# A routed two-layer network inside an attention kernel: expert units of 256 rows instead of 512, four to a chunk

## What is computed

```python
h = tokens(x)                                    # (32, 1024, 64)
h = layernorm(h + attention(h))                  # one head, softmax over 1024 keys
logits = h @ gate_w + gate_b                     # 8 experts
e = argmax(softmax(logits)); prb = softmax(logits)[e]
pos = running count of rows of expert e          # over all 32768 rows in order
kept = pos < C                                   # C = 1.25 * 32768 / 8
y = relu(h @ w1[e] + b1[e]) @ w2[e] + b2[e]      # 64 -> 256 -> 64
out = layernorm(h + nan_to_num(y * prb * kept))
```

## Time and profile before

| | us |
|---|---|
| median of 3 runs | 1235.28 (1235.03 to 1239.02) |
| the profiled execution, device time | 1234.83 |
| its span, first to last instruction | 1233.0 |
| TensorE busy | 1041.4 (84%), 5036 instructions |
| VectorE busy | 919.1 (75%) |
| ScalarE busy | 650.8 (53%) |
| POOL busy | 718.3 (58%) |
| mean granted TensorE clock | 0.938 |

### The profile page before, as it was taken

The page is one execution under the profiler, slowest core; times in us unless marked ns, Lnnn a source line. Parts: engine busy times, 40 slices in busy tenths (PEclk is TensorE's granted clock), DMA queues, the critical chain, the costliest instruction groups (busy, mean ns, idle before and its releaser), DMA issues.

```text
span 1233.0 us, 17442 instructions
## 1 busy us (share of the span) xinstructions
PE 1041.4 (84%) x5036; PEld 534.8 (43%) x5036; DVE 919.1 (75%) x1927; ACT 650.8 (53%) x880; POOL 718.3 (58%) x712
## 2 busy tenths in 40 slices
PE   3899999999999999999999999999989873345530
PEld 2455555555455555555554555554544431111210
DVE  4667778778989898988888988888888664535541
ACT  2355554555666666666666666666656541223320
POOL 0014555444676767666766676767675776536655
PEclk9999999999999999999999999999999976677775
DMA  5334433444444444444444443434351202222300
GB/s 122 88 77 124 105 91 76 111 112 100 106 109 107 106 102 107 105 106 104 105 106 109 99 117 94 123 93 124 76 126 35 70 16 75 74 61 72 89 12 2
DMA packets 102661, 112.02 MB, mean 91 GB/s; under 512 B 54350, under 2 KB 78919, under 8 KB 102566
## 3 DMA queue, kind: packets, MB, share of 16 engines
q1 hardware_dynamic: 85158, 93.78, 31.5%
q0 software_dynamic: 17408, 17.12, 4.6%
HBM read 42.20 MB, written 19.30 MB: 50 GB/s over the span
## 4 chain that ended last, share of the span: by engine, by line
PE 55%; DVE 25%; issue 9%; another core or an unknown queue 5%; ACT 2%; DMA 1%; POOL 1%; SPq 1%; POOLq 0%; DVEq 0%; ACTq 0%
PE p_u L562 15%; PE p_st L546 8%; DVE mx L929 8%; PE p_st L549 7%; PE p_sm L532 5%; PE p_misc L518 4%; PE p_misc L497 4%; PE p_misc L577 3%; PE p_misc L623 3%; PE p_misc L638 2%; DVE ld L980 1%; DVE b_o L1135 1%; DVE b_p L1084 1%; DVE b_n L1100 1%
## 5 line engine op out<-in xcount | busy, mean ns | idle before, releaser
L1263 POOL DMA_INDIRECT slots<-rows,idx x256 | 265.0, 1035 | 236.1 <-issue 147.2
L1275 POOL DMA_INDIRECT out<-b_o,b_ix x288 | 304.3, 1056 | 138.7 <-issue 77.6
L929 DVE TENSOR_REDUCE mx<-p_sm 128x1 f32<-128x1024 f32 x252 | 307.3, 1219 | 89.8 <-PE p_sm L532 82.5
L751 ACT ACTIVATE pT<-p_st 128x1024 f32<-128x1024 f32 x256 | 262.1, 1024 | 186.7 <-PE p_st L549 98.9
L562 PE MATMUL p_u<-pT,vv 128*64 128x512 f32 x1024 | 263.5, 614 | 0.0
L546 PE MATMUL p_st<-mQ,sK 128*128 128x512 f32 x512 | 183.6, 440 | 5.3 <-ACT pT L751 3.4
L549 PE MATMUL p_st<-mR,sR 72*128 72x512 f32 x512 | 161.1, 395 | 0.0
L532 PE MATMUL p_sm<-sK,mQ 64*128 64x512 f32 x252 | 139.9, 555 | 12.8 <-DVE mx L929 8.2
L532 PE MATMUL p_sm<-hi,mQ 64*128 64x512 f32 x252 | 139.8, 555 | 0.0
L546 PEld LDWEIGHTS p_st<-mQ,sK 128*128 128x128 f32 x512 | 79.4, 189 | 104.2 <-issue 79.4
L623 PE MATMUL p_misc<-b_xT,b_w 64*128 64x512 f32 x244 | 79.3, 730 | 34.1 <-issue 19.2
(11 more groups left out here) (181 smaller groups left out, 1492.8 us busy)
## 6 DMA issues: line engine op xcount, KB each, us to landing
mQ<-hi SPq DMA_DIRECT2D x64, 256.0 KB
b_in<-slots SPq DMA_DIRECT2D x72, 132.0 KB
b_x<-slots SPq DMA_DIRECT2D x72, 128.0 KB
sK<-hi SPq DMA_DIRECT2D x32, 256.0 KB
sK<-lo SPq DMA_DIRECT2D x32, 256.0 KB
mR<-lo SPq DMA_DIRECT2D x32, 256.0 KB
sR<-hi SPq DMA_DIRECT2D x32, 256.0 KB
xt<-in_x SPq DMA_DIRECT2D x32, 196.0 KB
```

Source lines behind the costliest of these rows:

```text
L751: act.activation(pT[k % 4][:, :], flat(p_st), ACT.Exp).then_inc(exp_done, 1)
L929: dve.tensor_reduce(mx[:, p, j:j + 1], flat(max_place(n, j)), AX.X, ALU.max).then_inc(max_done, 1)
L1263: pool.indirect_dma_start(slots, bass.IndirectOffsetOnAxis(ap=idx[:, p, j:j + 1], axis=0), rows[:, p, j, :], None, bounds_check=SLOTS - 1, ...
L1275: pool.indirect_dma_start(out_rows, bass.IndirectOffsetOnAxis(ap=b_ix[:, o, j:j + 1], axis=0), b_o[:, o, j, :], None, bounds_check=T - 1, ...
```

## The change

UNIT becomes 256 and a chunk holds four units (two pairs, v = 0 and 1), so a chunk still has 1024 rows. The last units of the experts are filled better, and NC = (128 + 8) / 4 = 34. HOST begins at step 6: 27 chunks inside steps 6 to 32, 7 after the attention (27 and 28 from the table of image 30, then 29 to 33). The first chunk takes its units from image 2's table, written in step 4. Each chunk now reads four table entries and issues 16 DMAs; `up` and `down` run twice as many matmuls of 256 columns; `rectify` does eight activations of 256 columns instead of four of 512 and waits for both pairs before the first; `sums_copy` does two instead of one. The tiles b_w1 and b_w2 get room for two pairs. Transposes, VectorE's work on a chunk and the scatters of a chunk keep their count and size. The diff, cut to its core:

```diff
-UNIT = 512
+UNIT = 256
+PAIRS = 2
+CT = PAIRS * UT
-NC = (NB * S // UNIT + E) // 2
-HOST = [*range(8, NB + 1)]
+NC = (NB * S // UNIT + E) // 4
+HOST = [*range(6, NB + 1)]
@@ image_of
     for n in (NB - 4, NB - 2):
-        if c < n - 3:
+        if c < n - 1:
             return n
-TAKEN = [2 * IMAGE.count(n) for n in TABLES]
+TAKEN = [4 * IMAGE.count(n) for n in TABLES]
@@ load_chunk
-                for u in range(2):
-                    named = sp.value_load(tab[0:1, 2 * c + u:2 * c + u + 1], min_val=0,
+                for u in range(2 * PAIRS):
+                    named = sp.value_load(tab[0:1, 2 * PAIRS * c + u:2 * PAIRS * c + u + 1], min_val=0,
                                           max_val=PACK * (E - 1) + DUMMY)
...
-                for u in range(2):
-                    sp.dma_start(b_x[:, r, :, u * D:(u + 1) * D], unit_rows(at[u])[:, :, 0:D])\
+                for k in range(2 * PAIRS):
+                    v, u = k // 2, k % 2
+                    t = slice(v * UT, (v + 1) * UT)
+                    sp.dma_start(b_x[:, r, t, u * D:(u + 1) * D], unit_rows(at[k])[:, :, 0:D])\
                         .then_inc(c_loaded[r], 16)
+                    sp.dma_start(b_in[:, r, u, t, :], unit_rows(at[k])).then_inc(c_loaded[r], 16)
+                    sp.dma_start(b_w1[u * D:(u + 1) * D, r, v, :],
+                                 w1[bass.ds(e[k], 1), :, :].rearrange("a k f -> (a k) f")).then_inc(c_loaded[r], 16)
+                    sp.dma_start(b_w2[:, r, v, u, :], w2[bass.ds(e[k], 1), :, :].rearrange("a k f -> (a k) f"))\
                         .then_inc(c_loaded[r], 16)
@@ up
-                for u in range(2):
-                    h = slice(u * D, (u + 1) * D)
-                    pe.matmul(place[:, u, :], b_w1[h, r, f * P:(f + 1) * P], b_xT[h, :], start=True, stop=True)\
-                        .then_inc(b_h_done, 1)
+                for v in range(PAIRS):
+                    for u in range(2):
+                        h = slice(u * D, (u + 1) * D)
+                        pe.matmul(place[:, u, v * UNIT:(v + 1) * UNIT], b_w1[h, r, v, f * P:(f + 1) * P],
+                                  b_xT[h, v, :], start=True, stop=True).then_inc(b_h_done, 1)
@@ down
+                for v in range(PAIRS):
+                    for f in range(HB):
+                        for u in range(2):
+                            last = pe.matmul(place[u * D:(u + 1) * D, v * UNIT:(v + 1) * UNIT],
+                                             b_w2[:, r, v, u, f * D:(f + 1) * D], b_h[:, f, u, v, :],
+                                             start=(f == 0), stop=(f == HB - 1))
@@ rectify
                 for u in range(2):
-                    act.wait_ge(b_h_done, 2 * HB * c + 2 * f + u + 1)
-                    act.activation(b_h[:, f, u, :], place[:, u, :], ACT.Relu,
-                                   bias=b_w2[:, r, u, HB * D + f:HB * D + f + 1]).then_inc(b_relu, 1)
+                    act.wait_ge(b_h_done, 2 * PAIRS * (HB * c + f) + 2 * (PAIRS - 1) + u + 1)
+                    for v in range(PAIRS):
+                        act.activation(b_h[:, f, u, v, :], place[:, u, v * UNIT:(v + 1) * UNIT], ACT.Relu,
+                                       bias=b_w2[:, r, v, u, HB * D + f:HB * D + f + 1]).then_inc(b_relu, 1)
@@ sums_copy
-                act.activation(b_yT[:, :], banks(c)[2], ACT.Identity, bias=b_w1[:, r, FF:W1C])\
-                    .then_inc(b_yT_ready, 1)
+                act.activation(b_yT[:, 0, :], banks(c)[2][:, 0:UNIT], ACT.Identity, bias=b_w1[:, r, 0, FF:W1C])
+                act.activation(b_yT[:, 1, :], banks(c)[2][:, UNIT:2 * UNIT], ACT.Identity,
+                               bias=b_w1[:, r, 1, FF:W1C]).then_inc(b_yT_ready, 1)
```

More of the change, by code:

```diff
@@ L193, in build @@
         tab = sb("tab", [P, UNITS], U32)
-        b_w1 = sb("b_w1", [P, NBUF, W1C])
-        b_w2 = sb("b_w2", [P, NBUF, 2, W2C])
-        b_in = sb("b_in", [P, NBUF, 2, UT, ROW])
-        b_x = sb("b_x", [P, NBUF, UT, 2 * D])
-        b_xT = sb("b_xT", [P, UNIT])
-        b_h = sb("b_h", [P, HB, 2, UNIT])
-        b_yT = sb("b_yT", [P, UNIT])
+        b_w1 = sb("b_w1", [P, NBUF, PAIRS, W1C])
+        b_w2 = sb("b_w2", [P, NBUF, PAIRS, 2, W2C])
+        b_in = sb("b_in", [P, NBUF, 2, CT, ROW])
+        b_x = sb("b_x", [P, NBUF, CT, 2 * D])
+        b_xT = sb("b_xT", [P, PAIRS, UNIT])
+        b_h = sb("b_h", [P, HB, 2, PAIRS, UNIT])
+        b_yT = sb("b_yT", [P, PAIRS, UNIT])
         b_eps = sb("b_eps", [P, 1])
@@ L266, in turned_back @@
         def turned_back(c):
-            return back_place(c).rearrange("p (j u d) -> p u j d", j=UT, d=D)
+            return back_place(c).rearrange("p (j u d) -> p u j d", j=CT, d=D)
         w_loaded = sem("w_loaded")
@@ L465, in _ @@
             for r in range(NOUT):
-                sp.wait_ge(b_scattered[r], 16 * NT * NC // NOUT)
+                sp.wait_ge(b_scattered[r], 16 * NT * len(range(r, NC, NOUT)))
         @block.tensor
@@ L514, in project @@
                     if chunk_of(n - 1) is not None:
-                        pe.wait_ge(b_relu, 2 * HB * (chunk_of(n - 1) + 1))
+                        pe.wait_ge(b_relu, 2 * PAIRS * HB * (chunk_of(n - 1) + 1))
                 for j in range(4):
@@ L583, in rows_turn @@
                 r = c % NBUF
-                pe.wait_ge(c_loaded[r], 128 * (c // NBUF) + 128)
+                pe.wait_ge(c_loaded[r], 128 * PAIRS * (c // NBUF + 1))
                 if c < INSIDE:
@@ L590, in rows_turn @@
                     pe.wait_ge(b_xT_ready, c)
-                for j in range(UT):
+                for j in range(CT):
                     last = pe.transpose(banks(c)[0][:, j * P:(j + 1) * P], b_x[:, r, j, :], c_id[:, :])
@@ L599, in turn_back @@
                     pe.wait_ge(b_p_ready, c)
-                for j in range(UT):
-                    last = pe.transpose(place[:, j * P:(j + 1) * P], b_yT[:, j * P:(j + 1) * P], c_id[:, :])
+                for j in range(CT):
+                    last = pe.transpose(place[:, j * P:(j + 1) * P], b_yT[:, j // UT, j % UT * P:(j % UT + 1) * P], c_id[:, :])
                 last.then_inc(b_back_done, 1)
@@ L615, in up @@
                 if c < INSIDE and f == 1:
-                    pe.wait_ge(b_relu, 2 * HB * c + 2)
+                    pe.wait_ge(b_relu, 2 * PAIRS * HB * c + 2 * PAIRS)
                 if c == INSIDE and f == 1:
@@ L619, in up @@
                 if c > INSIDE:
[L620 to L624 removed]
+                    pe.wait_ge(b_relu, 2 * PAIRS * HB * (c - 1) + 2 * PAIRS * (f + 1))
+                for v in range(PAIRS):
[3 more added lines that the diff above has]
+                                  b_xT[h, v, :], start=True, stop=True).then_inc(b_h_done, 1)
             def down(c):
                 r, place = c % NBUF, banks(c)[2]
[L629 removed]
+                pe.wait_ge(b_relu, 2 * PAIRS * HB * (c + 1))
                 if c < INSIDE:
@@ L635, in down @@
                     pe.wait_ge(b_yT_ready, c)
-                for f in range(HB):
-                    for u in range(2):
-                        last = pe.matmul(place[u * D:(u + 1) * D, :], b_w2[:, r, u, f * D:(f + 1) * D],
-                                         b_h[:, f, u, :], start=(f == 0), stop=(f == HB - 1))
+                for v in range(PAIRS):
[4 more added lines that the diff above has]
+                                             start=(f == 0), stop=(f == HB - 1))
                 last.then_inc(b_y_done, 1)
@@ L770, in xT_copy @@
                 if c >= 1:
-                    act.wait_ge(b_h_done, 2 * HB * c)
-                act.activation(b_xT[:, :], banks(c)[0], ACT.Copy).then_inc(b_xT_ready, 1)
+                    act.wait_ge(b_h_done, 2 * PAIRS * HB * c)
+                act.activation(b_xT[:, :, :].rearrange("p v r -> p (v r)"), banks(c)[0], ACT.Copy)\
+                    .then_inc(b_xT_ready, 1)
             def rectify(c, f):
@@ L1084, in weigh @@
                 dve.tensor_tensor(b_p[:, :, :].rearrange("p (u j) d -> p u j d", u=2), turned_back(c),
-                                  b_in[:, r, :, :, D].unsqueeze(3).broadcast_to([P, 2, UT, D]), ALU.mult)\
+                                  b_in[:, r, :, :, D].unsqueeze(3).broadcast_to([P, 2, CT, D]), ALU.mult)\
                     .then_inc(b_p_ready, 1)
```

7 lines of the change are left out of this document (removed).

## The result

The changed kernel takes **1248.49 us** (median of 4 runs, 1243.88 to 1252.59), the kernel before on the same chip 1235.15 (1227.25 to 1239.02): a ratio of 1.0094, 95% interval 1.0055 to 1.0133. It is 0.9% slower; I had said 1199 us and faster with a chance of 0.88. The prediction was wrong in its sign, and the time lies outside its range.

What follows compares the result with a forecast made beforehand. TensorE, 97% busy, was taken to set the pace inside the attention, SP the rounds after it. Span 1233.0 + 11.5 + 2.5 - 49.9 = 1197.1, with device time and median offset 1199 us; range 1184 to 1226.

Steps and rivals of the forecast that it cites:

- Steps 6 to 9, +11.5: Inside the attention: two more steps carry a chunk, so these four take 123.1 us for 111.6, +11.5 us.
- Matmuls, nothing: `up` and `down` in twice as many pieces: next weights load beside a running product, so 0 us.
- Narrow activations, +0.1 us a step: ScalarE's rectify, eight activations of 256 columns for four of 512, delays the exponent little: 0.1 us a step.
- SP, nothing: SP's 16 issues and four value loads inside a step finish before the next step's copies are late: 0 us.
- After the attention, -49.9: Last chunks: earlier loads, SP-paced rounds of 14.5 us and a last chunk without slow stretch or POOL backlog: -49.9 us.
- (a): Rival after the attention: SP's doubled instructions meet slow stretches every round, 4 to 5 us more each; 1217 to 1225 us, chance 0.22.
- (c): Rival inside the steps: narrow activations delay the exponent 1.2 us, weight loads exposed 0.95 a step; 1250 us, chance 0.08.
- (b): Rival after the attention: the slow stretch shrinks too and rounds run at 13.4 us; 1185 us, chance 0.10.

Runs made afterwards that it cites:

- narrow: Kernel before (8 issues a chunk) with up, down, rectify and sums_copy in pieces of 256 columns; 1186.83 us on chip E, ratio 0.9965.
- late2: Changed kernel with SP's load in odd steps issued at about +21 us instead of +13; 1221.14 us on chip F, ratio 0.9953 to the kernel before.
- nobx_after: Changed kernel without loads of b_x, rows_turn reading b_in, 12 issues a chunk; 1207.92 us on chip B, ratio 0.9790 to the kernel before.
- nobx_after2: Changed kernel without loads of b_x, 12 issues a chunk, run again on chip D; 1216.92 us, ratio 0.9835 to the kernel before.

## Why the prediction was wrong

**Steps 6 to 9, +11.5:** nearly right without stretches (122.47 - 111.95 = 10.5), 15.9 on chip A, where step 9 already took 35.9.

**Matmuls, nothing:** right. TensorE is busy 608.96 us in steps 10 to 29 of narrow on chip E, 609.8 before, with 320 matmuls more. The rule of the Trainium skill ("TensorE: Matmul & The Clock Gate", section "The mechanism") would have put the added weight loads beside it; the trace does not agree with the sentence that I went by. The same section also names a second way, a load into the background weight buffer, which I left out; the trace doesn't speak against that one.

**Narrow activations, +0.1 us a step:** no cost seen without stretches: the steps take 31.16 (narrow) and 31.18 (changed) on E and C, and narrow is 3.3 us faster in all than the kernel before; where it gains them isn't shown. Eight at 475 ns took 3.1 us of ScalarE in two groups of 1.57.

**SP, nothing: this is the step that failed.** I wrote that "odd steps have more room" and that "a loss of a few us a step on SP costs nothing". The count was nearly right: 16 issues, done in time, though 0.72 us apart and not 0.68 (from the first to the eighth start in the earlier trace rows pass 5.06 us, seven gaps), so that a load takes 11.3 us and not 10.9. What I left out is that in a slow stretch not SP alone but ScalarE and VectorE stand still too, so the question was not SP's room but what TensorE would be waiting for when one comes. The term was 0 and measured +1.4 us a step. On chip A the ten odd steps took 340.12 us, on C 305.36. TensorE was busy 314.63 and 303.80 of them: so of the 34.8 us, 23.9 are idle time, 25.5 for 1.6, and 10.8 are more busy time of TensorE, 8.7 of these in the four steps with a lower clock.

**After the attention, -49.9:** -30.0 on chip A. The forecast, counted from the start of step 31, had chunk 29's load at 102.4 and the pace at 14.5; measured 101.5 and, where nothing is slow, 14.2 to 14.6. Behind the last load I had 43.7 us, measured 45.8 (1247.92 - 1202.08). The missing part is chunk 30's load: 28 us for 11, between two full-speed rounds. I had planned for one slow load and got another. In sum I had 215 us for this part, so 24 of slow time beside the 191.3 that it takes without stretches; it lost 44 to them, as many as the kernel before. Without stretches it is 30 us shorter than in narrow, the closest to the kernel before with a trace there (221.1).

**The rivals.** (a) named the right mechanism, SP's doubled instructions in slow stretches, but only after the attention, and against it I set that SP's issues kept 0.68 in steps 10 to 29. I had read that from step 22. Step 15 of the same trace has a slow stretch within its load:

```profile
476.84 1.63 SPq L423 DMA_DIRECT2D b_in<-slots  x1
478.70 0.53 SPq L424 DMA_DIRECT2D b_w<-in_w  x1
479.42 0.44 SPq L426 DMA_DIRECT2D b_w<-in_w  x1
481.67 0.87 SPq L421 DMA_DIRECT2D b_x<-slots  x1
```

That step took 30.85 us all the same. An 8-issue load ends 17 to 20 us into an odd step, the changed one 24 to 27. (c) had the right place, the exponent in the second half of the step and TensorE behind it, and its time, 1250, was nearly met; that was luck, for its cause was wrong: eight activations take 3.1 us where (c) had 5.0 and I had 3.0, and the exponent is late in a stretch for which the trace names no engine. (b), shrinking stretches, is what chips C and E show, for another reason.

The range failed because every term came from one execution on one chip. The 45 us that slow stretches take from the kernel before, the largest uncertain quantity in its profile, were in none of my cases absent, and in none inside the steps. (The chances listed for the faster cases add up to 0.89, not 0.88.)

**Open:** what makes a slow stretch, and why it is on some chips. That SP, ScalarE and VectorE go on together and that DMA is at 43 GB/s in the long one speaks against a queue's own load and against bandwidth. POOL, which scatters through them, may have a part in them: in the kernel before one ended with POOL's run of scatters, and the runs without scatters met no chip with stretches. I know only what goes with the loss inside the steps: a long load of SP, small instructions, and their place.

## What to carry to other kernels

Stalls for which the trace names no engine are a cost with a size of its own: sum them, ask if they are there on another chip, and if a change moves queue work next to the critical engine, price the case that they come along. Moving DMA issues away from the bound engine's tightest microseconds can be worth as much inside a step as removing a quarter of them: 31.73 us (late2) and 31.80 to 31.99 (nobx_after, nobx_after2) for 32.92 to 33.06. In the whole time the removal was worth more here, a ratio of 0.979 to 0.984 for 0.995. A trace is of one run: see where that run lies among the others before its steps are compared with another kernel's. An edit judged on one chip may have the other sign on the next.

## What the runs showed of the hardware

At least five chips, one program, two behaviours: 1190 us on two, 1226 to 1236 on the others, with the same instructions and bytes. The difference lies in stretches in which register moves of 29 ns take up to 704; SP, ScalarE and VectorE go on within 0.11 us of each other, while POOL keeps its pace. TensorE's clock fell from 2.4 to 1.2 GHz after a pause of 2.25 us in step 17, before which it had been busy almost without a break, and stayed low for some 7 us, so the pause was paid for a second time, in longer matmuls; in step 29 a pause of 2.20 us left the clock at 2.4 GHz. And 256-column pieces of a matmul cost TensorE nothing: 608.96 us in 20 steps for 609.8.
